# Cross-attention and FFN turns taken in double steps of two tiles

## What is computed

```python
x = x + attn(layernorm(x), Wq, bq, Wk, bk, Wv, bv, Wo, bo)      # 16 heads of 128
x = x + xattn(layernorm(x), ctx, ctx, gamma)
x = x + ffn(layernorm(x), w1, w3, w2)

def xattn(q, k, v, gamma):              # B=4, D=512 rows, L=512 columns, 8 heads of 64 rows
    qk = einsum('bhdq,bhdl->bhql', qh, kh) / sqrt(64)
    return gamma * einsum('bhql,bhdl->bhdq', softmax(qk), vh)

def ffn(x, w1, w3, w2):                 # hidden 1365, weights made ternary
    return (silu(x @ w1q.T) * (x @ w3q.T)) @ w2q.T
```

## Time and profile before

| what | us |
|---|---|
| median of 3 runs | 1116.18 (1115.83 to 1116.68) |
| the profiled execution | 1116.88 |
| its span, first to last instruction | 1115.1 |
| span of one turn (of three) | 107.26 |
| from the last turn's start to the end | some 65 |

### The profile page before, as it was taken

How to read it: one execution, slowest core, us unless ns; L and a number is a source line. 1 busy time by engine, 2 the same in 40 slices (tenths; PEclk the granted TensorE clock), 3 DMA queues, 4 the chain that set the end, 5 groups by cost and what they waited for, 6 DMA issues and landing times.

```text
span 1115.1 us, 15853 instructions
## 1 busy us (share of the span) xinstructions
PE 1103.3 (99%) x5816; PEld 937.0 (84%) x5816; DVE 738.2 (66%) x1363; ACT 544.7 (49%) x1141; POOL 479.8 (43%) x420
## 2 busy tenths in 40 slices
PE   8999999999999999999999999999999999999998
PEld 6888887878888888888888888888888888888886
DVE  7555548786887679765525344679967976887532
ACT  3455673333243376667525142267727762775130
POOL 0322326440424265674353040158637762875130
PEclk9999999999999999999999999999999999999999
DMA  7555554534442733312630102461113211310100
GB/s 246 163 189 178 167 181 139 183 109 168 152 138 71 241 104 123 105 39 85 252 113 9 67 30 86 147 205 51 51 53 114 76 48 58 108 53 2 38 1 38
DMA packets 54664, 122.19 MB, mean 110 GB/s; under 512 B 10058, under 2 KB 10058, under 8 KB 52539
## 3 DMA queue, kind: packets, MB, share of 16 engines
q1 hardware_dynamic: 54586, 121.18, 33.3%
HBM read 103.32 MB, written 17.84 MB: 109 GB/s over the span
## 4 chain that ended last, share of the span: by engine, by line
PE 94%; DVE 3%; DMA 1%; issue 1%; ACT 1%; POOL 0%; SPq 0%; DVEq 0%; POOLq 0%
PE bank L175 19%; PE bank L176 19%; PE bank L177 19%; PE bank L581 7%; PE bank L582 7%; PE bank L539 5%; PE bank L597 4%; PE bank L596 4%; PE bank L563 3%; PE bank L564 3%; PE bank L549 2%; PE bank L550 2%; DMA x1d<-x_scratch 1%; PE bank L606 0%; DVE x3l L858 0%
## 5 line engine op out<-in xcount | busy, mean ns | idle before, releaser
L581 PE MATMUL bank<-x3h,w 128*128 128x512 f32 (+2 forms) x368 | 143.0, 392 | 0.4 <-DVE x3l L858 0.3
L1456 ACT ACTIVATE yh<-bank 128x512 fp32r<-128x512 f32 x64 | 38.1, 599 | 211.2 <-PE bank L177 211.1
L582 PE MATMUL bank<-x3l,w 128*128 128x512 f32 (+2 forms) x368 | 140.2, 384 | 0.0
L2106 POOL TENSOR_TENSOR wal<-raw_a,wah 128x512 fp32r<-128x512 f32 x44 | 61.6, 1430 | 131.8 <-ACT wah L1498 131.8
L938 POOL TENSOR_SCALAR pe_x<-pe_x,xri,gam 128x512 f32<-128x512 f32 x96 | 75.6, 788 | 78.4 <-DVE xri L777 75.9
L773 DVE TENSOR_REDUCE xmx<-bank 128x1 f32<-128x512 f32 x128 | 87.6, 686 | 32.4 <-PE bank L550 31.2
L175 PE MATMUL bank<-wah,gh 128*128 128x512 f32 x256 | 102.7, 401 | 0.0
L175 PE MATMUL bank<-yh,rh 128*128 128x512 f32 x256 | 100.6, 393 | 1.8 <-DVE xacc L1956 1.8
L2111 POOL TENSOR_TENSOR wbl<-raw_b,wbh 128x512 fp32r<-128x512 f32 x64 | 87.0, 1385 | 32.7 <-ACT wbh L1519 32.5
L176 PE MATMUL bank<-wal,gh 128*128 128x512 f32 x256 | 100.2, 391 | 0.0
L175 PE MATMUL bank<-wah,ph 128*128 128x512 f32 x256 | 100.1, 391 | 0.0
(11 more groups left out here) (173 smaller groups left out, 3009.9 us busy)
## 6 DMA issues: line engine op xcount, KB each, us to landing
raw_a<-in_wk SPq DMA_DIRECT2D x8, 1024.0 KB, 5.3
raw_b<-in_wq SPq DMA_DIRECT2D x8, 1024.0 KB, 6.1
raw_a<-in_wo SPq DMA_DIRECT2D x8, 1024.0 KB, 5.1
raw_b<-in_wvt SPq DMA_DIRECT2D x8, 1024.0 KB, 4.8
ternary_scratch<-wraw SPq DMA_DIRECT2D x24, 341.2 KB, 3.0
x1d<-x_scratch SPq DMA_DIRECT2D x48, 128.0 KB, 2.9
kd<-in_ctx SPq DMA_DIRECT2D x48, 128.0 KB, 3.0
w<-ternary_scratch SPq DMA_DIRECT2D x2, 2730.0 KB, 10.7
```

The lines of the kernel that those rows point to most:

```text
L581: pe.matmul(u_bank[w][0:m, cols], lhs, x3h[:, c, cols], start=c == 0, stop=False)
L582: mm = pe.matmul(u_bank[w][0:m, cols], lhs, x3l[:, c, cols], start=False, stop=c == CK - 1)
L2106: pool.tensor_tensor(wal[:, c, :], raw_a[:, c, :], wah[:, c, :].bitcast(F32), ALU.subtract).then_inc(s["wal_pool"], 1)
```

## The change

It goes through a turn in 16 double steps n = 2h + q/2, each with two tiles (h, q) and (h, q+1).

- The banks 0 and 1, 2 and 3 are made as two tensors of two banks. One reduction takes both score banks (`dve_max_two`), one copy and one subtraction take both transposed tiles (`act_px_two`, `dve_px_two`), one reciprocal two sums. The two exponentials and the two divisions stay single.
- TensorE does both scores, then both tiles' transposes, then in even steps a whole output (`pe_ret_whole`: eight matmuls of 512 columns) of head h-2, then its FFN pieces: one in even steps and in steps 1 and 15, two in the odd steps 3 to 13. `r_done` counts outputs, which in the turns are one each now.
- ScalarE does, in this order: tanh of the last piece of the step before, its gates, in odd steps the copy of two tiles, exponential q, tanh of the first piece where a step has two, exponential q+1, keys; in even steps it waits for the output of head h-2 and does the copy of two tiles; then queries and values.
- VectorE does: product of the last piece of the step before, reciprocals, maximum of two, query scaling, in even steps the output's additions, subtraction of two tiles, product of the first of two pieces, moments.
- GpSimd: the low part of the keys in step 2h and that of the queries in step 2h+1, behind the FFN's low part, with waits on its own earlier instructions. Values are copied in step 2h (before: single step 4h+2, for head 0 single step 1).
- At the turn's end the last transposes come in pairs and the last outputs whole, with five and six chunks of down-projection between.

```diff
+        two = [stack.enter_context(nc.psum_tensor(f"two{i}", [P, 2, 512], F32)) for i in range(2)]
+        bank = [t[:, k] for t in two for k in range(2)]
...
+        STEPS = 2 * XH
...
         def values_step(h):
-            return 4 * h + 2 if h else 1
+            return 2 * h
         def prep_step(h):
-            return 4 * h if 0 < h < XH - 1 else None
+            return 2 * h if 0 < h < XH - 1 else None
...
         def pieces(n):
-            if n < 0 or n >= S_TILES:
+            if n < 0 or n >= STEPS:
                 return range(0)
-            return range(U_PIECES * n // S_TILES, U_PIECES * (n + 1) // S_TILES)
+            first = n + max(0, min(n, STEPS - 2) // 2 - 1)
+            return range(first, first + (2 if n % 2 and 1 < n < STEPS - 1 else 1))
...
+        def pe_ret_whole(pe, m, b, h):
+            pe.wait_ge(s["t_free"], t_p(b, h, 3) + 1)
...
+            pe_wait(pe, "r_free", b * XH + h, 1)
+            for c in range(CK):
+                lhs = m.vts[:, h % 4, c, :]
+                pe.matmul(m.r[:], lhs, m.pxh[:, c, :], start=c == 0, stop=False)
+                mm = pe.matmul(m.r[:], lhs, m.pxl[:, c, :], start=False, stop=c == CK - 1)
+            mm.then_inc(s["r_ready"], 1)
...
         def pe_turn(pe, b, f, nxt):
...
+            for n in range(STEPS):
+                h, q = n // 2, n % 2 * 2
+                if b is not None:
+                    for k in (q, q + 1):
+                        pe_sx(pe, main, b, h, k)
+                    if h:
+                        for k in (q, q + 1):
+                            pe_pt(pe, main, b, h - 1, k)
+                    if h >= 2 and q == 0:
+                        pe_ret_whole(pe, main, b, h - 2)
+                if f is not None:
+                    for piece in pieces(n):
+                        pe_up(pe, f, piece)
             if f is not None:
                 pe_down(pe, f, 0, range(0, HC // 2))
             if b is not None:
-                pe_pt(pe, main, b, XH - 1, 2)
+                pe_ret_whole(pe, main, b, XH - 2)
+                pe_pt(pe, main, b, XH - 1, 0)
+                pe_pt(pe, main, b, XH - 1, 1)
             if f is not None:
                 pe_down(pe, f, 0, range(HC // 2, HC))
             if b is not None:
+                pe_pt(pe, main, b, XH - 1, 2)
                 pe_pt(pe, main, b, XH - 1, 3)
-                pe_ret(pe, main, b, XH - 1, 0)
             if f is not None:
-                pe_down(pe, f, 1, range(0, 3))
+                pe_down(pe, f, 1, range(0, HC // 2))
             if b is not None:
-                pe_ret(pe, main, b, XH - 1, 1)
+                pe_ret_whole(pe, main, b, XH - 1)
...
+        def act_px_two(act, b, h, q):
+            tiles, high, _ = shares(h, q)
+            act.wait_ge(s["t_ready"], t_p(b, h, q + 1) + 1)
+            act.activation(high, tiles, ACT.Copy).then_inc(s["pxh"], 2)
...
         def act_turn(act, b, f, nxt):
+            for n in range(STEPS):
+                h, q = n // 2, n % 2 * 2
                 if f is not None:
+                    for piece in pieces(n - 1)[-1:]:
+                        act_tanh(act, f, piece)
+                    for piece in pieces(n - 1):
+                        act_gate(act, f, piece)
+                if b is not None:
+                    if h and q:
+                        act_px_two(act, b, h - 1, q)
+                    elif h:
+                        act.wait_ge(s["t_ready"], t_p(b, h - 1, q + 1) + 1)
+                    act_exp(act, main, b, h, q)
+                if f is not None:
+                    for piece in pieces(n)[:-1]:
                         act_tanh(act, f, piece)
                 if b is not None:
+                    act_exp(act, main, b, h, q + 1)
                     if prep_step(h) == n:
                         act_keys(act, main, b, h + 1)
+                    if h >= 2 and q == 0:
+                        act.wait_ge(s["r_ready"], r_done(b, h - 2))
+                    if h and q == 0:
+                        act_px_two(act, b, h - 1, q)
+                    if prep_step(h) == n:
                         act_queries(act, main, b, h + 1)
+                    if h % 2 == 0 and values_step(h) == n:
+                        act_vt(act, main, b, h)
...
+        def dve_px_two(dve, b, h, q):
+            tiles, high, low = shares(h, q)
+            dve.wait_ge(s["pxh"], b * S_TILES + (4 * h + q + 2))
+            dve.tensor_tensor(low, tiles, high.bitcast(F32), ALU.subtract).then_inc(s["t_free"], 2)
+
+        def dve_max_two(dve, b, h, q):
+            dve.wait_ge(s["s_ready"], b * S_TILES + (4 * h + q + 2))
+            dve.reduce_max(xmx[:, q:q + 2], two[0][:], axis=AX, negate=True).then_inc(s["xmx"], 2)
...
         def dve_turn(dve, b, f, nxt, between=None):
+            for n in range(STEPS):
+                h, q = n // 2, n % 2 * 2
                 if f is not None:
+                    for piece in pieces(n - 1)[-1:]:
                         dve_up(dve, f, piece)
                 if b is not None:
                     if n:
+                        dve_rinv_two(dve, b, (n - 1) // 2, (n - 1) % 2 * 2)
+                    dve_max_two(dve, b, h, q)
                     if prep_step(h) == n:
                         dve_q(dve, main, b, h + 1)
+                    if q == 0 and h >= 2:
+                        dve_ret(dve, main, b, h - 2)
+                    if h:
+                        dve_px_two(dve, b, h - 1, q)
+                if f is not None:
+                    for piece in pieces(n)[:-1]:
+                        dve_up(dve, f, piece)
...
         def pool_turn(pool, b, f, nxt):
+            for n in range(STEPS):
+                h, q = n // 2, n % 2 * 2
+                if b is not None and n:
+                    for k in range(2):
+                        pool_prob(pool, main, b, (n - 1) // 2, (n - 1) % 2 * 2 + k)
+                if f is not None:
...
+                    for piece in pieces(n - 1):
+                        pool_up(pool, f, piece)
                 if b is not None:
+                    if prep_step(h) == n:
+                        pool_keys(pool, main, b, h + 1)
                     if prep_step(h) == n - 1:
+                        pool.wait_ge(s["xpn"], b * S_TILES + 2 * n)
+                        pool.wait_ge(s["gl2"], 1 + f * HC + pieces(n)[0] // 2)
+                        pool_queries(pool, main, b, h + 1)
```

More of the change, by code:

```diff
@@ L48 @@
 assert WP * WS * GROUPS == HID * C
-TANH_LAG, GATE_LAG = 1, 1
 RING_A = 4
@@ L744, in act_turn @@
             if b is not None:
-                for q in range(4):
-                    act_px(act, main, b, XH - 1, q)
+                for q in (0, 2):
+                    act_px_two(act, b, XH - 1, q)
                 if nxt is not None:
```

118 lines of the change are left out of this document (44 added, 74 removed).

## The result

The changed kernel takes 1150.8 us (median of four, 1149.4 to 1151.9), against 1116.0 for the kernel before on the same chip: a ratio of 1.031 (95% interval 1.030 to 1.032), 34.8 us slower. I had forecast 1135.0, in a range up to 1147.0: the direction held, the size did not. The profiled execution took 1150.85, with a span of 1149.0 against 1115.1.

What follows compares the result with a forecast made beforehand. The prediction took TensorE's issue (busy 99%) as the bound; late starts of 12.6, 6.9, 0.3 and 0.6 us, less 0.6 and 0.8, gave +19.0, so 1135 us for a median, in a range of 1126 to 1147.

Steps and rivals of the forecast that it cites:

- The new lock: Both score banks stay held from first score to exponential, so the next scores wait; transpose banks are locked likewise.
- A: Scores of step 1 wait for the two-tile maximum and exponential: +0.75 us a turn.
- B: Scores of step 2 wait behind tanh, FFN product, two-tile maximum and exponential: +1.55 us a turn.
- C: Transposes of step 3 wait for maximum, exponentials, keys, copy and subtraction: +1.9 us a turn.
- D: Loop's even steps: chains of 4, 8, 12 cost 0.75 each, 6.9 in all; those of 6, 10, 14 0.3 in all.
- The six half-hidden steps late too: Upper-bound case: the chains of steps 6, 10, 14, forecast only 0.05 us late, also run late.
- my dear end: Upper bound: dear two-tile instructions, steps 6, 10, 14 also late, 0.8 at each turn's end: +30, 1147 us.
- E: End of a turn: last whole output and the LayerNorm chain come late, 0.2 us a turn, 0.6 in all.
- Rival 4: Lateness feeds itself or the clock falls to half: 1141 us, with late steps 1145 to 1150; chance 0.14.
- D also in steps 6, 10, 14: Lateness case: the loop's even-step loss also hits these steps at 0.75 us each, VectorE behind throughout.
- Rival 1: All chains stay covered and large tiles save fixed latency, so the kernel is faster: 1113.9 us; chance 0.07.
- the rival was right in this: Experiments' rival theory: waits belong to queues as a whole and would turn up at the next step.

Runs made afterwards that it cites:

- The fill of the gap: Changed kernel plus twelve unread 256-column matmuls between scores and transposes of step 3 in each turn: 1148.0 us, ratio 1.029.
- the kernel with whole outputs alone: Kernel before, single steps kept, each head's output made whole between scores and transposes of tile 0 two heads later: 1138.6 us, ratio 1.021.
- The pair of kernels that differs only in this: Changed kernel with keys after copies, GpSimd's queries before FFN low part, FFN pieces moved earlier: two-tile maxima, copies, subtractions 1140.1 us; single-tile 1128.2 us.
- Order of keys: Changed kernel with ScalarE copying the two transposed tiles before the next head's keys in even steps (also called copy first): 1141.8 us, ratio 1.023.
- single maxima: Changed kernel with two maxima of one tile each in place of one of two tiles: 1138.5 us, ratio 1.020.
- single shares: Changed kernel with copies and subtractions of one transposed tile each, the maximum still of two tiles: 1136.1 us, ratio 1.018.
- queries first: Changed kernel with GpSimd's low part of the queries ahead of the FFN's low part, nothing else: 1151.1 us, ratio 1.031.
- the start's order: Changed kernel with the maximum ahead of the FFN product in steps up to 2 and head 0's values a step later: 1152.9 us, ratio 1.033.
- the spread: Changed kernel with FFN pieces laid 1, 2, 2, 2, 1, 2, 1, 2, 1, 2, 1, 2, 1, 1, 1, 0 over the steps: 1152.5 us, ratio 1.031.
- the best variant: Changed kernel with copies before keys, single-tile maxima, copies and subtractions, and GpSimd's queries before the FFN's low part: 1126.3 us, ratio 1.010.

## Why the prediction was right in direction and wrong in size

**The bound: right.** TensorE's issue sets the time; almost all that was lost is late starts of TensorE and its clock, and the account of the turns closes to 0.6 us of 34.5. The reading of the waits had a slip: of the 0.8, 0.3 and 0.2 us the 0.3 lies behind the three turns.

**Prices of operations: right.** 1.21 and 1.23 against 1.22 forecast, 1.02 against 1.0. Transposes 0.79 for eight and 0.32 to the next, 0.88 as forecast: pairing them saves nothing. Whole outputs earned 1.6 by the pitches, where I took 0.6 and gave 0 to 1.5: just outside.

**The new lock, A and B: right** in place, cause and size (3.5 and 4.9 against 3.2 and 4.7).

**C: mechanism right, term too small.** 2.29 against 1.9, in all three turns. The walk's order of operations is the one in the trace. What it lacked are handovers.

**D: the step that failed.** The mechanism was the right one, the size wasn't: 7.1 us forecast for all of D by the table, 18.0 measured. For the transposes behind the chains of steps 4, 8 and 12 I had 0.5; they are 0.86 to 0.93. For the chains of steps 6, 10 and 14 I had 0.05; they are 0.24 to 0.47. The walk ran "product to 1.5, maximum to 2.8, two exponentials to 4.2, keys to 4.7, copy to 5.7, subtraction to 6.95" and set operation on operation. The trace has 0.10, 0.10 and 0.14 between the engines, and in step 6 another 0.11 from the scores to the maximum. Where a chain misses by 0.05, that is no small error: it makes nine waits of 0.24 to 0.47 out of almost nothing. "The six half-hidden steps late too" was the right case, and it lay in my dear end only. There are nine such steps in three turns, not six, and nine times 0.75 is 6.75, not 6.9; the two slips cancel. The walk also leaves out the additions of the output ahead of the subtraction, which hold the chain of step 6 once the keys are out of the way. For GpSimd's queries I had 0.25; they are 0.48 in turns 2 and 3 and 0.83 to 0.87 in turn 1, each with 0.1 behind it. They hang on the same late chain, so its error counted twice. For the first turn's rests of the self-attention I had nothing.

**E:** 0.36 and 0.11 against 0.2, for the same reason, as far as the trace tells.

**Rival 4, the clock: happened, in one place and not by its route.** I gave the rival 0.14 and doubted it because the longest new wait was to be 1.9. It was 2.29, and the clock fell behind it twice, for 3.2 us in all. The fill of the gap shows that term by itself. It is not what I had for "D also in steps 6, 10, 14", which happened at half its price. The distance, then: 19.0, and 3.2 for the clock, 10.9 for the terms of D, 2.5 for A, B, C and E, less 1.9 for what was gained more than forecast, give 33.7. The Trainium skill, "TensorE: Matmul & The Clock Gate", section "HAM oscillation", warns that idle gaps which come again and again re-throttle the clock. The trace agrees in the case of step 3, with TensorE idle from 858 to 860 and a clock of 0.50 behind it, but not in every turn, and the gaps of that section are longer than this one. In the 1.5 us gaps of step 2 it didn't fall. My doubt rested on a wait of 1.9 being harmless; the kernel with whole outputs alone, where it fell behind 1.53, shows that this was no ground.

**Rival 1, the rule for large tiles.** The section cited for it speaks of operands in SBUF, and the maxima here read PSUM. VectorE did get cheaper, 84.7 to 83.1 us in a turn, and none of it reached the time. The pair of kernels that differs only in this says what the rule costs here: 11.9 us.

**Where the rest of the 34.8 lies.** Order of keys 9.1, single maxima 12.4, single shares 14.7, each undone alone, with 3.2, 1.6 and 3.2 of clock in them by the profiled executions. They overlap, since together (with the queries) they give 24.5. So the chains through locked banks are the cause, and the rival was right in this: a wait removed at one place came back in part at the next, with the copy first, single shares, queries first, the start's order and the spread. Some 10 us stay in the best variant: TensorE's late starts still sum to 2.7 us in each of the last two turns (B alone 0.97) and to 8.2 in the first, with four of 0.9 to 1.2 among them. I did not find a version with double steps that beats the kernel before. I also can't say from these runs whether one exists.

## What to carry to other kernels

An instruction that takes two tiles saved its engine some 0.06 us here and held both tiles' banks until the second one was through, so on a kernel whose TensorE is 99% busy it must be judged by the chain from matmul to freed bank, not by busy time. Walk that chain with the handovers in it (0.10 between VectorE and ScalarE, 0.14 to TensorE, 0.1 more behind each wait of TensorE), and treat a step that is late by less than their sum as late. An order mended at one step alone sent the wait to the next queue; mend the longest chain first and look again. And read the clock of each turn before you put a gain down to an edit.

## What the runs showed of the hardware that I had not expected

A small operation on VectorE waits for GpSimd. The four-element steps of the reciprocal root take 0.16 us; in the run with the queries first two of them took 1.13 and 1.20, and each ended where GpSimd's running instruction ended (759.67 + 1.30 = 760.97, 760.93 + 1.28 = 762.21):

```profile
759.86 1.13 DVE L169 SCALAR_TENSOR_TENSOR rstd<-ntmp,rstd 128x4 f32<-128x4 f32 x1
761.02 1.20 DVE L165 TENSOR_TENSOR ntmp<-rstd 128x4 f32<-128x4 f32 x1
...
759.67 1.30 POOL L1017 TENSOR_TENSOR gtl<-gf,gth 128x512 fp32r<-128x512 f32 x1
760.93 1.28 POOL L1005 TENSOR_TENSOR vts<-vd,vts 128x512 fp32r<-128x512 f32 x1
```

The Trainium skill, "SBUF — State Buffer", section "Who interferes with whom", says that a VectorE instruction with two inputs in SBUF contends with a GpSimd instruction that reads SBUF, and that the loser is blocked altogether. The trace agrees. VectorE's normalising of the queries grew likewise, from a mean of 564 ns to 787: it takes 0.53 to 0.54 where GpSimd stands (922.60 in the kernel before) and 0.97 beside its two divisions (892.94 in the changed one). In a chain with 0.5 us of slack this is a term that no operation's own price shows. With the queries first it is what makes the first turn's 2.16 out of 0.60, as far as the traces tell, though no run took it away.

In the changed kernel itself the first turn's longer waits for GpSimd (0.83 to 0.87, not 0.48) have a plainer reason. Two such operations stand ahead of the FFN's product in step 5 and take their usual time, 0.38 us from the first to the product, so the reciprocals and with them GpSimd come later:

```profile
752.83 0.15 DVE L165 TENSOR_TENSOR ntmp<-rstd 128x4 f32<-128x4 f32 x1
753.01 0.16 DVE L167 SCALAR_TENSOR_TENSOR ntmp<-ntmp,nvar 128x4 f32<-128x4 f32 x1
753.21 0.75 DVE L862 SCALAR_TENSOR_TENSOR gf<-uu,wscale,bank 128x512 f32<-128x512 f32 x1
```
